# A graph network's SAGE rounds with sums by rank of destination in place of scatters, and their gathers issued in one run

## The reference

```python
def sage_mean(h):                       # used by the first two stages
    agg = segment_sum(h[src], dst, N)
    return agg / maximum(count(dst), 1)[:, None]

# stage 0: two convolutions
def conv0(h, Wl, bl, Wr):
    o = sage_mean(h) @ Wl + bl + h @ Wr
    return relu(o / maximum(norm(o, axis=-1), 1e-12))
x = layernorm(x + conv0(conv0(x, ...), ...))
# stage 1: four convolutions
def conv1(h, Wl, Wr, b):
    return relu(sage_mean(h) @ Wl + h @ Wr + b)
x = layernorm(x + conv1(conv1(conv1(conv1(x)))))
# stage 2: attention over sources with a softmax per destination, four heads, norm of the row
# stage 3: transformer convolution with edge attributes, relu, batch norm over the nodes
```

## Time and profile before

| | us |
|---|---|
| median of three runs | 13674.33 |
| span of the profiled execution | 13680.0 |
| GpSimd busy | 7623.1 (56%) |
| Vector busy | 7443.6 (54%) |
| TensorE busy | 8579.7 (63%) |
| ScalarE busy | 4840.1 (35%) |
| setup, to the first gather | 1379 |
| six SAGE rounds, from first gather to first gather | 1214, 1273, 1209, 1201, 1200, 1260 |
| attention round, transformer round, last stage | 2352, 2017, 575 |

### The profile page before, as it was taken

How to read it: one execution, slowest core, us unless ns; L and a number is a source line. 1 busy time by engine, 2 the same in 40 slices (tenths; PEclk the granted TensorE clock), 3 DMA queues, 4 the chain that set the end, 5 groups by cost and what they waited for, 6 DMA issues and landing times. The chain is left out here.

```text
span 13680.0 us, 225686 instructions
## 1 busy us (share of the span) xinstructions
PE 8579.7 (63%) x38502; PEld 5910.7 (43%) x38503; DVE 7443.6 (54%) x21344; ACT 4840.1 (35%) x11306; POOL 7623.1 (56%) x9015
## 2 busy tenths in 40 slices
PE   6664666676656656665665666544444458888865
PEld 2121455455544445544454555333333334444444
DVE  7765455577732222222222555688888855555567
ACT  0000222366632222222222444455555532222257
POOL 2756666566656666666666666433433346666610
PEclk9975676666666666677666777666666668888876
DMA  7000555466645545554554666433343333333368
GB/s 312 2 4 12 165 170 165 158 204 206 202 152 170 167 147 174 172 165 151 174 171 149 212 211 207 157 123 118 118 125 120 122 108 111 118 112 117 108 205 279
DMA packets 1169328, 2072.18 MB, mean 151 GB/s; under 512 B 283837, under 2 KB 292600, under 8 KB 1156370
## 3 DMA queue, kind: packets, MB, share of 16 engines
q1 hardware_dynamic: 662400, 1128.29, 26.8%
q10 hardware_dynamic: 268534, 564.37, 10.8%
q0 software_dynamic: 238336, 378.92, 9.9%
HBM read 1358.91 MB, written 773.68 MB: 156 GB/s over the span
## 5 line engine op out<-in xcount | busy, mean ns | idle before, releaser
L668 POOL DMA_INDIRECT agg<-y_rows,s_idx x3136 | 3198.3, 1020 | 2715.4 <-issue 1150.7
L924 PE MATMUL o_bank<-w_r,h_t 128*128 128x128 f32 x12544 | 2551.3, 366 | 0.0
L924 PEld LDWEIGHTS o_bank<-w_r,h_t 128*128 128x128 f32 x12544 | 2177.2, 261 | 531.2 <-issue 530.4
L1081 ACT ACTIVATE h_t<-ht_bank 128x512 f32<-128x512 f32 (+1 forms) x1568 | 888.2, 593 | 3299.2 <-PE ht_bank L915 3155.4
L1650 DVE TENSOR_TENSOR total<-o_bank,agg_in 128x512 f32<-128x512 f32 (+1 forms) x1568 | 1032.5, 687 | 1803.5 <-DMA agg_in<-agg 1230.1
L921 PE MATMUL o_bank<-b_parts,ones_parts 3*128 3x512 bf16 (+1 forms) x1568 | 781.2, 498 | 1249.5 <-ACT h_t L1081 1021.7
L659 POOL DMA_INDIRECT gath<-node_a,g_idx x1176 | 1135.4, 965 | 635.6 <-issue 292.0
L818 PE MATMUL edge_bank<-ident,gath 128*128 128x128 f32 x2352 | 551.9, 380 | 1425.2 <-DMA gath<-node_a,g_idx 564.3
L915 PE MATMUL ht_bank<-ident,h_in 128*128 128x128 f32 x6272 | 1202.2, 354 | 376.4 <-issue 274.5
L1449 DVE COPY g_idx<-idx 128x8 int32 (+1 forms) x784 | 151.1, 193 | 2208.8 <-DMA gath<-node_a,g_idx 948.1
L915 PEld LDWEIGHTS ht_bank<-ident,h_in 128*128 128x128 f32 x6272 | 1017.2, 188 | 591.4 <-issue 505.2
(11 more groups left out here) (271 smaller groups left out, 14815.1 us busy)
## 6 DMA issues: line engine op xcount, KB each, us to landing
agg_in<-agg SPq DMA_DIRECT2D x1560, 256.0 KB
node_a<-h_out ACTq DMA_DIRECT2D x780, 256.0 KB
h_in<-node_a SPq DMA_DIRECT2D x780, 256.0 KB
node_x<-h_out ACTq DMA_DIRECT2D x392, 256.0 KB
node_b<-h_out ACTq DMA_DIRECT2D x392, 256.0 KB
h_in<-node_x SPq DMA_DIRECT2D x390, 256.0 KB
h_in<-node_b SPq DMA_DIRECT2D x390, 256.0 KB
agg<-zeros ACTq DMA_DIRECT2D x96, 1024.0 KB
```

Source lines behind the costliest of these rows:

```text
L668: pool.indirect_dma_start(agg[order(r)], bass.IndirectOffsetOnAxis(s_idx[q][:, k:k + 1], 0), y_rows[q][:, k, :], None, bounds_check=N - 1, ...
L924: last = pe.matmul(o_bank[s][0:p, j * P:(j + 1) * P], h_t[s][:, j, 0:p], w_r[r][:], start=False, stop=j == RPP - 1, skip_group_check=True)
L1081: act.activation(h_t[s][:, :, 0:p], ht_bank[s][:].rearrange("p (j n) -> p j n", j=RPP)[:, :, 0:p], ACT.Copy).then_inc(ht_ready[s], 1)
```

## The change

In the six SAGE rounds nothing is scattered to the aggregate. Setup gives each destination that has an edge a rank, counted from 0 in order of destination. Then:

- The gathered tile is not turned. Vector builds for each tile a 128x128 matrix `hot_rank` (edge by rank counted from the tile's first, with the value one over the count), and TensorE multiplies it with the tile into the block's bank at the column `starts[k]`, which it loads into a register. The bank is cleared by a 512-wide product with zeros first. This gives the means by rank, features in partitions. Vector copies them to SBUF and adds the carry-over of the last block's rank to the first column (`means`).
- The product with `w_l` stays. ScalarE copies the bank whole. SyncE stores the 512 rows to `rank_rows` in DRAM from the block's first rank (`write_rows`), one block after the other, since the second overwrites rows of the first. `before_units` waits for both.
- A unit has its nodes in windows of 128. For each of a group's four windows SyncE loads the 128 rows of `rank_rows` that end with the window's last rank (`load_ranks`: four values from SBUF to registers in one call, then four DMAs of 64 KB). Vector builds 0/1 matrices `hot_node` (rank by node of the window), and TensorE adds their product to `o_bank`, after bias and `h @ w_r`. Vector's add of the aggregate goes. The `relu` tails read the bank directly.
- So that a window of 128 nodes is one partition tile, all node arrays get another layout: row `(g p j)` holds node `(g j p)`. ScalarE's queue copies `x` into it at the start (57 DMAs, ahead of the copies of the weights), and the last stage's stores undo it (rows of 512 bytes).
- Setup gains `build_ranks`, `take_ranks` and `rank_bounds`, and in each block of both sort passes two one-hots of 784 columns and two of 128, with two products each, which put the nodes of each window in the order of rank.
- GpSimd has only gathers in the SAGE rounds, with no `pause` between them. The attention and transformer rounds keep scatters and pauses. `keep` is loaded for these two only.

The diff, cut to its core ("..." marks what is left out):

```diff
-                def before_units(i, r=r):
+                def before_units(i, r=r, kind=kind):
+                    rows = rows_out if kind == SAGE else scattered
                     for q in range(2):
-                        sp.wait_ge(scattered[q], scattered.at(r, i))
+                        sp.wait_ge(rows[q], rows.at(r, i))
                     sp.sem_inc(sp_turn, 1)
...
+                def write_rows(i, r=r):
+                    for q in range(2):
+                        start = sp.value_load(row_starts[0:1, bass.ds(block_of(i, q, r), 1)], min_val=P, max_val=P + EPAD)
+                        sp.wait_ge(y_ready[q], y_ready.at(r, i + 1))
+                        sp.sem_inc(sp_turn, 1)
+                        sp.wait_ge(rows_out[1 - q], rows_out.at(r, i + q))
+                        sp.sem_inc(sp_turn, 1)
+                        sp.dma_start(rank_rows[bass.ds(start, BLOCK)].rearrange("(c p) f -> p c f", p=P),
+                                     y_rows[q][:]).then_inc(rows_out[q], 16)
...
+                def load_ranks(u, s, r=r):
+                    _, ends = nc.values_load_multi_w_load_instructions(
+                        rank_ends[0:1, bass.ds(first_window(u, s), RPP)], engines=[mybir.EngineType.SP], min_val=0, max_val=EPAD)
+                    sp.wait_ge(mm_ready[s], mm_ready.at(r, u))
+                    sp.sem_inc(sp_turn, 1)
+                    for j in range(RPP):
+                        sp.dma_start(agg_in[s][:, j, :], rank_rows[bass.ds(ends[j], P)]).then_inc(ranks_loaded[s], 16)
...
@@ -701,18 +797,9 @@
                     continue
                 for q in range(2):
                     next_gathers(q, 2)
-                    pause(first_pause + q)
                 with pool.Fori(0, PAIRS - 2) as i:
                     for q in range(2):
-                        next_scatters(q, i + 1)
-                        pause(i * 4 + (first_pause + 2 + q))
-                    for q in range(2):
                         next_gathers(q, i + 3)
-                        pause(i * 4 + (first_pause + 4 + q))
-                for n in (PAIRS - 1, PAIRS):
-                    for q in range(2):
-                        next_scatters(q, n)
-                        pause(first_pause + PAUSES - 4 + 2 * (n - PAIRS + 1) + q)
...
+                    def nodes_of_windows(b, x):
+                        pe.wait_ge(window_hot[x], b + n * BLOCKS + 1)
+                        pe.matmul(o_bank[0][:], hot_slot[x], hot_window[x][:, 0:DIGITS], start=False, stop=False, skip_group_check=True)
+                        pe.matmul(pe_bank[1][:, 0:WINDOWS - DIGITS], hot_slot[x], hot_window[x][:, DIGITS:WINDOWS], start=False, stop=False,
+                                  skip_group_check=True).then_inc(window_used[x], 1)
...
                 def sage_turn(i, q, r=r):
+                    _, starts = nc.values_load_multi_w_load_instructions(
+                        tile_starts[0:1, bass.ds(block_of(i, q, r) * CPB, CPB)], engines=[mybir.EngineType.PE],
+                        min_val=0, max_val=BLOCK - P)
+                    pe.wait_ge(run_ready[q], run_ready.at(r, i))
+                    pe.matmul(pe_bank[q][:], no_ones[:], no_ones[:].unsqueeze(1).to_broadcast([P, CPB, P]), start=True, stop=False,
+                              skip_group_check=True)
+                    pe.wait_ge(rank_hot_ready[q], rank_hot_ready.at(r, i + 1))
                     pe.wait_ge(gathered[q], gathered.at(r, i + 1))
-                    pe.wait_ge(run_ready[q], run_ready.at(r, i))
                     for k in range(CPB):
-                        last = pe.transpose(pe_bank[q][:, k * P:(k + 1) * P], gath[q][:, k, :], ident[:])
+                        last = pe.matmul(pe_bank[q][:, bass.ds(starts[k], P)], gath[q][:, k, :], hot_rank[q][:, k, :],
+                                         start=False, stop=k == CPB - 1, skip_group_check=True)
                     last.then_inc(gt_ready[q], 1)
...
+                def sage_unit(u, r=r):
+                    ahead = not isinstance(u, int) or u + 1 <= UNITS
+                    for s in range(2):
+                        if ahead:
+                            turned(u + 1, s)
+                        pe.wait_ge(node_hot_ready[s], node_hot_ready.at(r, u + 1))
+                        pe.wait_ge(ranks_loaded[s], ranks_loaded.at(r, u + 1))
+                        for j in range(RPP):
+                            last = pe.matmul(o_bank[s][:, j * P:(j + 1) * P], hot_node[s][:, j, :], agg_in[s][:, j, :],
+                                             start=False, stop=j == RPP - 1, skip_group_check=True)
+                        last.then_inc(mm_ready[s], 1)
+                    if ahead:
+                        for s in range(2):
+                            own_rows(u + 1, s)
...
+            x_to = x_in[0:whole].rearrange("(g p j) f -> j g p f", j=RPP, p=P)
+            for g in range(0, GROUPS, COPIED):
+                for j in range(RPP):
+                    act.dma_start(x_to[j, g:g + COPIED], x_from[j, g:g + COPIED]).then_inc(x_copied, 16)
...
                     for q in range(2):
                         act.wait_ge(yp_ready[q], yp_ready.at(r, i + 1))
-                        act.wait_ge(scattered[q], scattered.at(r, i))
-                        for k in range(CPB):
-                            last = act.activation(y_rows[q][:, k, :], pe_bank[2 + q][:, k * P:(k + 1) * P], ACT.Copy,
-                                                  scale=inv[:, bass.ds(block_of(i, q, r), 1), k])
-                        last.then_inc(y_ready[q], 1)
+                        act.wait_ge(rows_out[q], rows_out.at(r, i))
+                        act.activation(wide(y_rows[q]), pe_bank[2 + q][:], ACT.Copy).then_inc(y_ready[q], 1)
...
+                    act.wait_ge(out_ready[s], out_ready.at(r, u + 1))
...
+                        act.dma_start(out[first + P:N], h_out[s][0:LASTN - P, 1, :]).then_inc(stored[s], 16)
+                    else:
...
+                        for x in range(2):
+                            k = 2 * n_pass + x
+                            dve.wait_ge(window_used[x], b + n_pass * BLOCKS + 1)
+                            dve.tensor_scalar(hot_slot[x], iota_f[:, 0:P], slot_t[:, bass.ds(b, 1), k], node_t[:, bass.ds(b, 1), k],
+                                              ALU.is_equal, ALU.mult)
+                            dve.tensor_scalar(hot_window[x], window_no, window_t[:, bass.ds(b, 1), k], None,
+                                              ALU.is_equal).then_inc(window_hot[x], 1)
...
+                def rank_hot(i, q, r=r):
+                    dve.wait_ge(gt_ready[q], gt_ready.at(r, i))
+                    b = table_block(i, q, r)
+                    for k in range(CPB):
+                        last = dve.tensor_scalar(hot_rank[q][:, k, :], node_no[:], local[:, bass.ds(b, 1), k], inv[:, bass.ds(b, 1), k],
+                                                 ALU.is_equal, ALU.mult)
+                    last.then_inc(rank_hot_ready[q], 1)
...
+                def means(i, q, r=r):
+                    b = block_of(i, q, r)
+                    at = dve.value_load(last_ranks[0:1, bass.ds(b, 1)], min_val=0, max_val=BLOCK - 1)
+                    dve.wait_ge(gt_ready[q], gt_ready.at(r, i + 1))
+                    dve.wait_ge(yp_ready[q], yp_ready.at(r, i))
+                    dve.wait_ge(run_ready[1 - q], run_ready.at(r, i + q))
+                    dve.tensor_copy(mean_t[q][:, 1:BLOCK], pe_bank[q][:, 1:BLOCK])
+                    dve.scalar_tensor_tensor(mean_t[q][:, 0:1], mean_t[1 - q][:, bass.ds(at, 1)], goes_on[:, bass.ds(b, 1)],
+                                             pe_bank[q][:, 0:1], ALU.mult, ALU.add).then_inc(run_ready[q], 1)
...
+                def node_hot(u, r=r):
+                    for s in range(2):
+                        dve.wait_ge(mm_ready[s], mm_ready.at(r, u))
+                        of = node_of[:, bass.ds(first_window(u, s), RPP)]
+                        dve.tensor_tensor(hot_node[s], node_no[:].unsqueeze(1).to_broadcast([P, RPP, P]),
+                                          of.unsqueeze(2).to_broadcast([P, RPP, P]), ALU.is_equal).then_inc(node_hot_ready[s], 1)
```

More of the change, by code:

```diff
@@ L121, in gnn_kernel @@
     soft_rounds = [R_GAT, R_TR]
+    sum_rounds = [r for r in range(NR) if ROUNDS[r][1] not in ("relu", "relu_ln")]
     all_edges = list(range(NR))
@@ L400, in width, with out_group, first_window @@
         def width(u, s):
[L401 removed]
+            return P
+        def out_group(t, u, s):
+            if isinstance(u, int):
+                first = u * UNIT + s * GROUP
+                return t[first:first + GROUP].rearrange("(j p) f -> p j f", p=P)
+            every = t[0:UNITS * UNIT].rearrange("(u h j p) f -> u h p j f", h=2, j=RPP, p=P)
+            return every[bass.ds(u, 1), s].rearrange("o p j f -> (o p) j f")
+        def first_window(u, s):
+            per = 2 * RPP
```

(52 more changed lines are left out.)

323 lines of the change are left out of this document (275 added, 48 removed).

## The result

The changed kernel takes 14966 us (median of four runs, 14953 to 14983) against 13673 of the kernel before: 1.0944 times as long, 95% interval 1.0928 to 1.0959. Predicted were 15400, with 13950 to 16450 as the range. The profiled execution spans 14953.9 us, 1274 more than before.

What follows compares the result with a forecast made beforehand. SyncE's queue was taken to bound the changed SAGE rounds at 28.3 us a pair. Span 13680 + 1394 (rounds) + 115 (copies) + 39 (ranks) + 110 (one-hots) + 70 (last stage) = 15408, predicted as 15400; range 13950 to 16450.

Steps and rivals of the forecast that it cites:

- GpSimd is no bound any more: SAGE rounds: without eight scatters and four closings GpSimd needs 10 us a pair of blocks, 490 us a round.
- TensorE at 21 to 27 us a pair: SAGE relu rounds: added rank products bring TensorE from 15.0 to 21 to 27 us a pair, close behind SyncE.
- SyncE's pair is 28.3 us: SAGE rounds: loads and writes of ranks, h loads and schedule take SyncE 28.3 us a pair, against 24.5 before.
- The sixth round at 1523: Last SAGE round: a relu round's 1405 us plus 118 for loading residual rows, 1523 us.
- First and second round at 1415 and 1598: First two SAGE rounds: 10 us added in the first, 75 in the second for Vector's long chain; 1415 and 1598 us.
- Copies of x, +115: Setup: 57 copies of x on ScalarE's queue delay the weight copies TensorE waits for, +115 us (+60 to +200).
- One-hots in the sort passes, +110: Setup: window one-hots on Vector lengthen pass 0 by 98 us and pass 1 by 12, +110 (0 to 290).
- Ranks and keep, +39: Setup: Vector steps and TensorE round trips for ranks +54 us, load of keep gone -15, together +39 (20 to 70).
- Last stage, +70, and the others 0: Last stage: stores in 512-byte pieces cost 0.7 us a unit, +70 us (0 to 150); GAT and transformer rounds unchanged.
- SyncE being cheap: Rival, SAGE rounds: a group's four values cost 0.7 us, a write lands in 2.5, kernel faster at 13400 us; chance 0.15.
- TensorE at 1.2 GHz: Rival, SAGE rounds: TensorE stays at the low clock, 32 us a pair, 16400 us in all; chance 0.14.

Runs made afterwards that it cites:

- a_combo_pause: Changed kernel without load_ranks checks, loads of h on ScalarE's queue, copies of x behind weight copies, pauses behind gathers restored: 13599 us, 0.9943 of the kernel before.

## Why the prediction was right

Forecast was slower by 1726, 1394 of it by one mechanism, SyncE's queue in the SAGE rounds. It was slower by 1293, and 1073 of it lie in these rounds, by that mechanism. Its steps:

- *GpSimd is no bound any more.* Right: its gathers wait for TensorE, which waits for loads of ranks. It is busy 376 us a round, not near 490; that number had the 0.30 between two DMAs in it.
- *TensorE at 21 to 27 us a pair.* Too high: 970 to 986 us in the relu rounds are 20, at a granted clock of 0.81 to 0.83.
- *SyncE's pair is 28.3 us.* 26.4 was measured; with the 18 us for start and drain, 28.7 and 27.2. The largest miss is the price of a group: the loads of ranks take 14.9 for 16.6. In the pair shown above, the eight DMAs of two groups took 5.66 us; four take 3 x 0.52 + 0.33 = 1.89, so 1.88 lie between the groups, and a group is 3.77, not 4.14. The issue at 0.52 was right, so it is the 2.0 for four values that was too much. The writes of ranks are 6.2 for 7.2, as one lands in 2.4 in the median. Two terms were too small: the loads of h are 3.4 for 2.4, 0.8 of it waiting for TensorE, which the prediction put at nothing, and the schedule 2.5 for 2.1. Relu rounds: 1405 predicted, 1316 to 1332 measured.
- *The sixth round at 1523*: 1526, but that agreement hides two errors, since the relu rounds, on which it was built, were 80 too long. The residual loads and what follows them cost some 200, not 118. SyncE waits 112 us at L644 there against 72, which is 40 of the 80. What makes the rest was not tested.
- *First and second round at 1415 and 1598*: 1395 and 1538. The first round is 71 longer than a relu round, for 10; SyncE waits for TensorE there before its loads of h, 126.5 us in all against 40.4. The second is 12 longer than the sixth, for 75. So neither term was right. The two waits named here, of the sixth round (8458 to 9984) and of the first (1553 to 2949):

```profile
SPq L644 <- DMA rank_rows<-y_rows: 112.2, 49, 3.6
```

```profile
SPq L659 <- PE ht_bank L1062: 126.5, 110, 7.3
```

- *Copies of x, +115.* The transpose came 152 us later. With the copies moved back (a_combo_pause), the first record scatter stands at 248 instead of 388, 140 earlier, and the first gather 113 earlier (1442 against 1555), as the copies then lengthen the first pass by some 27. So 140 for 115: right in size, and the largest part of the setup's 175.
- *One-hots in the sort passes, +110.* Wrong: 5. The step that failed was to take the idle 1.2 us a block of Vector as turns of the loop. The pass is paced by GpSimd's record scatters (each pass as long between its first and last scatter as before, within 2 us), and Vector had that slack. The prediction named this cover as what could make it wrong, and didn't use it. The earlier trace rows have it already: 369 us for 385 scatters and 0.30 behind each are 485 of the 512.
- *Ranks and keep, +39.* About right. The first record scatter is 181 later than in the kernel before (388 against 206); less the 140 of the copies, 41 are left for the ranks, for 54. From the last record scatter to the first gather it is 36 us, not 47: 11 less, for the 15 of `keep`.
- *Last stage, +70, and the others 0.* The last stage is 597 for 575, +22; the transformer round is 8 shorter, the attention round 12 longer.

So the mechanism held, and most terms were too dear: the rounds by 321, the one-hots by 105, the last stage by 48; only the copies were too cheap, by 25. The total is right by that mechanism. The near hits of the first and the sixth round are luck, as their terms were off in opposite directions.

The rivals: SyncE being cheap needed 2.8 us a group, and it is 3.7. TensorE at 1.2 GHz is out, the granted clock was 0.75 to 0.83, above the 0.66 to 0.70 of the earlier trace rows. That SyncE is the bound is shown, not only argued: without moving a byte, the two edits that only shorten its queue (checks, and who issues the loads of h) took 747 and 671 us on the loud chips, and with the setup edit 1391 on the quiet one (14990 with the pauses alone, 13599 with all), of which 114 are the setup's. On the quiet chip neither of the two was run by itself.

The Trainium skill (Runtime: NRT & Kernel Launch, Instruction fetch mechanics) has some 200 ns for each register loaded, in bulk too; it says so of register loads that the runtime puts in. For these loads from SBUF the trace does not agree: four registers took 0.30 us, one 0.27. What makes four values dear is their checks. The Trainium skill (DMA: Bandwidth & Descriptors, Rules for kernel authors) also says to coalesce many small transfers. The trace agrees in what matters here: an issue costs SyncE 0.333 us for 64 KB as for 256 KB.

## What to carry to other kernels

A queue that issues DMAs is an engine with a budget: when a scatter is replaced by loads at computed places, add up each value loaded, each check and each issue per step, and look where the same transfers could be issued by a queue with time to spare. Work that goes to an engine in a stretch that another one paces is free until it reaches that pace, so ask what paces the stretch first. A short wait in the engine that sets the pace is not waste before it has been measured without it, on more than one chip.

## What was not expected of the hardware

- On two of three chips register steps on SyncE's queue took 0.7 us instead of 0.04 now and then (1305 in one execution), all of them in or just behind an uninterrupted run of GpSimd's indirect DMAs; Vector's and ScalarE's queues had 128 and 65. On the third chip no kernel had any, the changed one with the same runs of GpSimd among them.
- The kernel before is 6 per cent slower on those chips (14501 against 13673), the changed one 17 per cent (17462 against 14966). Why they differ stays open, and so does whether pauses between the gathers would help the changed kernel there.
- Without the pauses, with runs of sixteen indirect DMAs, the kernel before was 10 per cent slower on the loud chips, though each DMA by itself kept its 0.94 to 1.02 us.
